# Local attention on TensorE: queries 0 to 63 as one 64x64 tile instead of two 64x32 tiles

## The reference, cut to what matters

```python
HEADS, DIM_HEAD, WINDOW = 16, 64, 32
q, k, v = split(shift_tokens(x) @ Wqkv[i])          # 128 tokens, 16 heads of 64
q, k = l2norm(q) * qs, l2norm(k) * ks               # then rotated
# four windows of 32 queries; each sees its own and the previous window's 32 keys
sim = einsum('bhwie,bhwje->bhwij', bq, look(bk)) * 8.0
sim = where((it < jb) | (it > jb + 32) | (jb == -1), -max, sim)
out = einsum('bhwij,bhwje->bhwie', softmax(sim), look(bv))
x = out.reshape(b, n, 1024) @ Wo[i] + x
x = ffn_layer(shift_tokens(x), ...) + x             # layer norm, gated, 341 hidden
```

## Time and profile before

| | |
|---|---|
| median of 3 runs | 2962.42 us (2959.99 to 2966.43) |
| the profiled execution, its own time | 2970.78 us |
| its span | 2968.9 us |
| mean granted TensorE clock | 0.965 of full speed |
| PE, DVE, ACT, POOL busy | 91%, 67%, 59%, 44% |
| instructions on PE (loads, matmuls) | 41474, 41474 |

### The profile page before, as it was taken

The page is one execution under the profiler, slowest core; times in us unless marked ns, Lnnn a source line. Parts: engine busy times, 40 slices in busy tenths (PEclk is TensorE's granted clock), DMA queues, the critical chain, the costliest instruction groups (busy, mean ns, idle before and its releaser), DMA issues.

```text
span 2968.9 us, 103175 instructions
## 1 busy us (share of the span) xinstructions
PE 2692.8 (91%) x41474; PEld 1980.6 (67%) x41474; DVE 1985.6 (67%) x4762; ACT 1741.6 (59%) x3705; POOL 1296.9 (44%) x1689
## 2 busy tenths in 40 slices
PE   7799999999999999999999999999897877999875
PEld 5556666666666666666666666666776866998655
DVE  6777766777677766777777777776566667555562
ACT  5566766777677666777677677766442255222542
POOL 5555454455455545545445554554231055000660
PEclk9899999999999999999999999999897999999997
DMA  2100001000100001000100000000002000000004
GB/s 78 63 13 14 14 15 50 15 14 11 54 15 11 14 15 49 14 14 12 54 15 12 13 16 15 13 13 15 4 4 76 0 5 5 1 0 1 5 3 142
DMA packets 50940, 66.56 MB, mean 22 GB/s; under 512 B 24505, under 2 KB 30084, under 8 KB 49284
## 3 DMA queue, kind: packets, MB, share of 16 engines
q1 hardware_dynamic: 50820, 64.87, 7.8%
HBM read 38.23 MB, written 1.05 MB: 13 GB/s over the span
## 4 chain that ended last, share of the span: by engine, by line
PE 49%; DVE 22%; POOL 13%; issue 9%; ACT 4%; POOLq 1%; SPq 1%; DMA 1%; DVEq 0%; ACTq 0%
PE ps L798 6%; POOL area L1450 6%; PE ps L759 5%; DVE area L1831 4%; POOL area L1444 4%; PE ps L720 4%; DVE area L1799 4%; DVE area L1801 4%; PE ps L726 4%; PE ps L902 3%; PE ps L890 3%; PE ps L889 3%; PE ps L825 2%; PE ps L791 2%; DVE ssq L1785 2%
## 5 line engine op out<-in xcount | busy, mean ns | idle before, releaser
L1062 ACT ACTIVATE area<-ps 64x128 f32<-64x128 f32 (+5 forms) x1532 | 774.6, 532 | 492.7 <-PE ps L726 131.2
L1444 POOL TENSOR_TENSOR area<-area 128x512 f32<-128x512 f32 x384 | 488.3, 1272 | 823.5 <-DVE area L1801 823.5
L1450 POOL TENSOR_TENSOR area<-area,rnq 128x512 f32<-128x512 f32 x384 | 396.3, 1043 | 14.4 <-ACT rnq L1189 0.6
L720 PE MATMUL ps<-lw,area 128*128 128x512 f32 x768 | 401.3, 626 | 0.7 <-ACT area L1062 0.7
L1785 DVE TENSOR_REDUCE ssq<-area 128x8 f32<-128x512 f32 x384 | 261.2, 680 | 37.4 <-ACT area L1171 24.4
L726 PE MATMUL ps<-ident,area 128*128 128x128 f32 x1536 | 242.7, 281 | 31.4 <-POOL area L1450 30.3
L1857 DVE SCALAR_TENSOR_TENSOR area<-ps,lcol,area 128x128 f32<-128x128 f32 (+1 forms) x288 | 83.0, 344 | 276.4 <-ACT area L1212 272.1
L1801 DVE TENSOR_TENSOR area<-ps,table 128x512 f32<-128x512 f32 x384 | 260.9, 679 | 0.0
L1799 DVE TENSOR_TENSOR area<-ps,table 128x512 f32<-128x512 f32 x384 | 259.0, 675 | 0.0
L1171 ACT ACTIVATE area<-ps 128x512 f32<-128x512 f32 x384 | 227.1, 592 | 45.9 <-PE ps L720 45.9
L1262 ACT ACTIVATE area<-ps 128x256 f32<-128x256 f32 x208 | 79.7, 383 | 245.7 <-PE ps L890 245.7
(11 more groups left out here) (278 smaller groups left out, 5722.3 us busy)
## 6 DMA issues: line engine op xcount, KB each, us to landing
lvm<-area SPq DMA_DIRECT2D x384, 65.0 KB, 2.0
lw<-in_wqkv SPq DMA_DIRECT2D x6, 1536.0 KB
area<-in_moe_w SPq DMA_DIRECT2D x32, 256.0 KB, 3.0
lw<-in_wout SPq DMA_DIRECT2D x6, 512.0 KB
ctxT<-in_ctxT SPq DMA_DIRECT2D x64, 38.5 KB, 1.8
lw<-in_wff SPq DMA_DIRECT2D x6, 341.0 KB
lw<-in_moe_g SPq DMA_DIRECT2D x1, 1152.0 KB
lw<-in_moe_u SPq DMA_DIRECT2D x1, 1152.0 KB
```

The lines of the kernel that those rows point to most:

```text
L720: nc.tensor.matmul(ps[s][:, j, :], xsT[s], wqkv[w.p][:, j * 512:(j + 1) * 512], start=True, stop=True).then_inc(l_qk_ps, 1)
L1062: return nc.scalar.activation(dst, src, ACT.Identity if kw else ACT.Copy, **kw)
L1444: pool.tensor_tensor(QR[s][:, cols], QR[s][:, cols], RA[s][:, cols], ALU.add).then_inc(l_rsum, 1)
L1450: pool.tensor_tensor(rows, rows, rnq[s][:, 8 * j:8 * j + 8, None].to_broadcast([S, 8, LD]), ALU.mult).then_inc(l_qkn, 1)
```

## The change

Queries 0 to 63 (windows 0 and 1), which use the same key blocks and the same values, become one group of 64 stationary columns; windows 2 and 3 stay groups of 32. It applies to `scores` and to `probs_values`. Each call issues 24 matmuls instead of 32: for each head pair, two on 64x64 tiles and then four on 64x32 tiles.

```diff
+            groups = ((0, 64, 0), (64, 32, 1), (96, 32, 2))
+
-            def near_keys(s, c, odd, n):
+            def near_keys(s, c, odd, g):
                 keys = QKT[s][64 * odd:64 * odd + 64, INNER + c * S:INNER + (c + 1) * S]
                 blocks = keys.rearrange("p (b n) -> p b n", n=WINDOW)
-                return blocks[:, 2:0:-1, :] if n == 2 else blocks[:, n // 2 * 2:n // 2 * 2 + 2, :]
+                return (blocks[:, 0:2, :], blocks[:, 2:0:-1, :], blocks[:, 2:4, :])[g]
+
+            def near_values(s, h, odd, g):
+                rows = slice(64 * odd, 64 * odd + 64)
+                return (LV[s][rows, 0, h, :], LVM[s][rows, h, :], LV[s][rows, 1, h, :])[g]
...
                 for c in range(4):
-                    for n in range(4):
+                    for lo, size, g in groups:
                         for odd in range(2):
-                            out_rows = slice(32 * n, 32 * n + 32)
-                            cols = slice((4 * m + c) * S + 32 * n, (4 * m + c) * S + 32 * n + 32)
+                            cols = slice((4 * m + c) * S + lo, (4 * m + c) * S + lo + size)
                             last = nc.tensor.matmul(
-                                ps[s][out_rows, 2 * m + odd, c * 64:(c + 1) * 64].rearrange("p (b n) -> p b n", n=WINDOW),
-                                QKT[s][64 * odd:64 * odd + 64, cols], near_keys(s, 4 * m + c, odd, n),
+                                ps[s][lo:lo + size, 2 * m + odd, c * 64:(c + 1) * 64].rearrange("p (b n) -> p b n", n=WINDOW),
+                                QKT[s][64 * odd:64 * odd + 64, cols], near_keys(s, 4 * m + c, odd, g),
                                 start=False, stop=(c == 3), skip_group_check=True)
...
                 for c in range(4):
-                    for n in range(4):
+                    for lo, size, g in groups:
                         for odd in range(2):
-                            rows, out_rows = slice(64 * odd, 64 * odd + 64), slice(32 * n, 32 * n + 32)
-                            at = (4 * m + c) * S + 32 * n
-                            v = LVM[s][rows, 4 * m + c, :] if n == 2 else LV[s][rows, n // 2, 4 * m + c, :]
-                            last = nc.tensor.matmul(ps[s][out_rows, 2 * m + odd, c * 65:(c + 1) * 65],
-                                                    LPT[s][rows, at:at + 32], v, start=True, stop=True)
+                            at = (4 * m + c) * S + lo
+                            last = nc.tensor.matmul(ps[s][lo:lo + size, 2 * m + odd, c * 65:(c + 1) * 65],
+                                                    LPT[s][64 * odd:64 * odd + 64, at:at + size], near_values(s, 4 * m + c, odd, g),
+                                                    start=True, stop=True)
```

## The result

The changed kernel takes 3394.0 us (median of 4 runs, 3392.23 to 3397.31) against 2964.4 us of the kernel before beside it (4 runs, 2960.0 to 2971.2): a ratio of 1.1448, 95% interval 1.1423 to 1.1473. It is slower by 430 us, where 443 were forecast (3406 us; range 3090 to 3490).

The account below looks back on a forecast made before the run. PE was taken to bound the kernel: 4.87 us more a period, less 0.15 and 0.1 hidden, gives 4.62, times 96 samples 443 us. Added to the profiled 2970.8 us: 3414, less 8.4: 3406 us; range 3090 to 3490.

Parts of the forecast that it names:

- What bounds: In the local transformer PE is busy 19.19 of a period's 19.85 us, so added PE time delays the rest.
- The price of a change: On PE, each change of tile shape costs 0.09 us on top of the streaming.
- B: Between 64x64 and 64x32 matmuls on PE nothing is emptied, so faster: 2900 to 2931, say 2920 us; chance 0.10.
- C: On PE, groups of different shape await each other's streaming without emptying the array: about 3090 us; chance 0.06.
- The call: A call of `scores` takes 2.02 us instead of 0.79, a head pair 0.505; two calls of `probs_values` 4.04 instead of 1.63.
- PEld was to show idle pauses before every group: Expected sign in the profile: PEld idle before each group of matmuls; no size given.
- the matmuls taken out save nothing: In both functions, removing 8 of 32 matmuls a call saves nothing, since issue no longer limits.
- The cover: Of 4.87 us added a period on PE, 0.15 and 0.1 are absorbed by waits, leaving 4.62.
- At the loop's branch: Before L714, one period in two, a wait of 0.31 us absorbs added time: 0.15 us a period.
- the wait before the first outputs' transposes: Between L720 and L791, PE's wait of 0.1 us for the outputs on DVE absorbs added time.
- rival D: The pauses on PE also bring the clock down, to 0.89: about 3640 us; chance 0.03.
- Rival E: Whole kernel within 0.2% of before, B's gain hidden or balanced by small losses; chance 0.03.

Follow-up runs that it names:

- e5_scores_only: The changed kernel with the 64x64 group in the scores only, the value products as in the kernel before: 3176.3 us, ratio 1.0717.
- e6_values_only: The changed kernel with the 64x64 group in the value products only, the scores as in the kernel before: 3168.2 us, ratio 1.0686.
- e4_all_wide: The changed kernel with windows 2 and 3 also one 64x64 tile, leaving window 3's attention out: 2938.9 us, ratio 0.9920 to the kernel before.
- e7_scores_together: The kernel before with a sample's two calls of scores back to back, both masks first, then the tokens' transpose: 3059.5 us, ratio 1.0321.

## Why the prediction was right

**What bounds.** "Time added on PE in `scores` delays the rest of the period": shown by e5_scores_only, and for the value products by e6_values_only.

**The price of a change.** The step that the trace of before could not show, a change between two small shapes, came out at the 0.09 us of the four changes that have the full array on one side. By the Trainium skill, "TensorEngine Tiling (Array Packing)", Tiling Modes, a change of tiling mode drains TensorE. The trace agrees between the two small shapes, in both directions: 0.15 us between starts, of which 0.053 is streaming. Rivals B and C, that nothing is emptied between small tiles, fall by these pauses and the straight line of 7, 4 and 1 changes.

**The call.** 2.03 us measured against 2.02, a pair 0.51 against 0.505, the two calls of value products 4.08 (1029.97 to the next line's 1034.05) against 4.04. One sign of the forecast did not come: PEld was to show idle pauses before every group, but its idle time before L764 is listed 201 times for 9216 loads, about once a call. A load record lasts 0.10 us and more, and several overlap, so that the pauses are seen in the starts of the matmuls and not there. That the matmuls taken out save nothing is right where shapes are mixed. In one shape they do save: 0.17 us a call in e4_all_wide, for 16 matmuls fewer.

**The cover.** Forecast were 0.25 us a period of hidden time and 4.62 us in all. The spans differ by 3395.5 - 2968.9 = 426.6 us, 4.44 a sample. With the measured calls, PE's work grew by 2 x (2.03 - 0.79) + (4.08 - 1.63) = 4.93 us a period, 473 us in all, where 4.87 and 468 were forecast. So 47 us were hidden or saved elsewhere, and not 24: this term was half of what it should have been. The forecast came within 17 us in spite of it because the term is small, and because the 5 us missing in the work offset a part. Waits of PE from 160 us to the local transformer's end, in the kernel before and then after:

```profile
PE ps L791 <- DVE area L1831: 16.7, 91, 0.2
PE ps L784 <- issue: 12.2, 3, 4.1
PE ps L714 <- issue: 9.0, 27, 3.9
PE ps L714 <- DVE xw L1781: 3.0, 12, 0.3
```

```profile
PE ps L802 <- ACT area L1066: 23.8, 95, 0.3
PE ps L714 <- issue: 3.7, 1, 3.7
```

The outputs' transposes in one period before, and the projection in one period after:

```profile
1014.59 0.66 PE L791 MATMUL ps<-ident,area 128*128 128x128 f32 x4 [0.18 <-DVE area L1831]
1015.10 2.05 PE L798 MATMUL ps<-lw,area 128*128 128x128 f32 x16
```

```profile
1036.30 2.05 PE L802 MATMUL ps<-lw,area 128*128 128x128 f32 x16 [0.25 <-ACT area L1066]
```

The 47 us can be put together as an estimate. At the loop's branch 38 short waits before L714 are gone, 0.31 us each: 12 us, where 15 were forecast. From L720 behind the value products to the projection it was 1015.10 - 1012.68 = 2.42 us and is 1036.30 - 1034.05 = 2.25: 0.17 less, 16 us, where 10 were forecast. The forecast took the wait before the first outputs' transposes, and had neither the 0.18 us before the second ones, which is gone too, nor the new wait of 0.25 us of the projection for ScalarE's copy. Three of the four pauses near 4 us at `issue` are gone, which the sum had not counted: 12 us. Why they went, no run shows. The last part is the clock.

**The clock** (rival D) did not suffer from the pauses of 0.1 us inside a busy engine: it is 1.00 over the stretch, after 0.99 before. It did fall now and then in both kernels. Stretches of 40 us of the kernel before and 10 us of the kernel after, in the form of the earlier trace rows:

```profile
800.00:840.00 40.00, 35.45 (x669) 24.16 (x667) 26.51 (x57) 24.22 (x50) 16.64 (x17) 0.91 0.27 86
```

```profile
1290.00:1300.00 10.00, 10.00 (x108) 5.91 (x107) 3.28 (x7) 3.34 (x6) 0.00 (x0) 0.51 0.12 28
```

Before, it fell six times, four of them right behind the pauses near 4 us (here behind 3.90 us in front of L714, which starts at 807.10); after, twice. Adding up what the stretches of 40 us lack to full clock gives about 16 us before and 10 after, so some 5 us more are saved. All four parts make 45 of the 47 us. At the lower of the two levels, 1.2 GHz, a call of the changed `scores` lasts 3.17 us (at 1290.18) instead of 2.10.

Rival E is out by the size of the loss.

## What to carry to other kernels

Count the changes of tile shape on TensorE before counting matmuls: here each cost 0.14 us, of which 0.09 is the pause itself. That is as much as fourteen of the records that the merge was to save, at 10 ns each. Merge small matmuls into wider ones only if the whole run of them then has one shape, or at least sort a run by shape; mixing inside the inner loop was the dearest of the three orders tried. And before moving work together to save changes, look at what it covers: in e7_scores_together, 0.19 us saved uncovered a round trip to ScalarE of 1.07 us and made the masks wait for another of its copies.

## What the runs showed of the hardware that was not expected

Between shapes that both use small tiles, the pause is the same as to and from the full array (starts 0.15 us apart with 0.053 us of streaming). That holds in both directions, although the next group always begins in columns that the last matmul of the group before did not use. In one shape, wide tiles are not slower: 32 records of 64x64 last 0.69 us against 0.86 for 64 of 64x32.
